# The last stage of a fused eight-stage kernel: expert products in two rounded parts each, the down product turned round

## The chip, the cores and the metric

The kernel is one program on one core of a Trainium2 chip. The time is that of the device, in microseconds (us), for one execution. Several executions are timed, and one more is recorded by the hardware profiler, which gives the trace that is read here.

## The reference

A residual stream x of 4 x 512 = 2048 tokens by 128 passes through eight layers, each `x = x + layer(layernorm(x))`: gated linear attention, a routed feed-forward layer, low-rank attention, a second routed layer, a block with generated weights, a ternary feed-forward layer, full attention with 16 heads, and a mixture of experts. Only the last one is changed. It has 8 experts with 512 slots each, and every token goes to its two best experts:

```
scores = softmax(xt @ wg);  gates_k, idx_k = top_k(scores, 2), gates normalized to sum 1
disp[e, slot] += token rows, in order of choice and token; rows past 512 slots are dropped
h   = relu(einsum('ecd,edh->ech', disp, w1) + b1)     # 128 -> 512
out = einsum('ech,ehd->ecd', h, w2) + b2              # 512 -> 128
y   = sum over k of gates_k * out[idx_k, slot]
```

## The kernel before

The eight stages run one after the other. Residual rows stay in on-chip memory (`sh.x`); each stage has a block of instructions for every engine, in an order written out by hand, and the engines meet through semaphores: `then_inc` counts up when an instruction is done, `wait_ge` holds an engine's queue until a count is reached. Everything behind a wait on the same engine waits too.

The last stage is `dispatched_ffn` (L3051). Its course:

- *Routing.* Layer norm, logits (`route`), softmax and the choice of two experts, and counts that give every token its slot (`give_slots`, `keep`), by all engines for four chunks of tokens. The two expert weight matrices and b2, repeated over the partitions, are loaded at the stage's start by three transfers (L3132 to L3134).
- *Dispatch.* GpSimd issues 32 indirect transfers (L3167) that put rows of 128 tokens each into the slots in device memory (`disp`).
- *Expert loop.* For each expert e, SyncE loads its 512 rows (L3140). TensorE turns them (`turn`, L3228, four transposes of 128x128 in full precision), ScalarE copies the result to `rowsT` (L3275). `up(e)` (L3237) has four products, one for each 128 of the 512 hidden columns: w1's 128x128 stands in the array, 512 turned rows stream through. Full precision needs two records for each such product in the trace. ScalarE applies bias and relu (L3281) from one of two banks `ps_up` into `hidden`. `down(e)` (L3247) has sixteen smaller products, in which 128x128 of the hidden values stand and 128 columns of w2 stream, so that the result has the slots on the partitions. VectorE adds b2 (L3393) and GpSimd stores the 512 rows with four indirect transfers (L3182), to the places by token that VectorE has worked out (L3390, L3391).
- TensorE's order is up(0), turn(1), up(1), turn(2), down(0), up(2), turn(3), down(1), and so on to up(7), down(6), down(7). VectorE's order for each expert is places, then the y of this expert.
- *End.* When all stores have landed SyncE loads the rows back (L3146), VectorE adds them by their gates to the residual (L3402), and the last block stores x.

Of the kernel before, what the change touches and what calls it, by code (L numbers as in the profile page):

```python
# [19 lines left out]
P = 128  # L20
# [3029 lines left out]

def dispatched_ffn(sh, stage, n_exp=8, hid=512, top=2):  # L3051

# [8 lines left out]
    U = top * NT  # L3061
    n_up, n_slot = hid // P, cap // P
    assert cap == S
    GROUP, K16 = 4, top * n_exp
    with ExitStack() as ctx:  # L3065
# [5 lines left out]
        ps_y = [bank(f"y{i}") for i in range(2)]  # L3071
        ps_route, ps_count = [bank("route"), ps_up[0]], [bank("count"), ps_up[1]]
        ROW = D + 1
# [8 lines left out]
        second = sb("second_choice", [P, n_exp, n_slot])  # L3082
        place = sb("place", [P, 2, n_slot])
        place_i = sb("place_int", [P, 2, n_slot], U32)
        tri = sb("tri", [P, P], BF16)
# [21 lines left out]
        rows = sb("rows", [P, 3, n_slot, ROW])  # L3107
        rowsT = sb("rowsT", [P, 2, S])
        hidden = sb("hidden", [P, 2, n_up, S])
        y = sb("y", [P, 2, n_slot, D])  # L3110
        back = sb("back", [P, U, D])
        w1, w2 = sb("w1", [P, n_exp * hid]), sb("w2", [P, n_exp * hid])
        b2 = sb("b2", [P, n_exp * D])
        s_w1, s_w2 = sem("w1_loaded"), sem("w2_b2_loaded")
        s_const = sem("constants_made")
# [12 lines left out]
        @block.sync  # L3128
        def _(sp):
            sh.load_next(sp, stage)  # L3130
            n = n_exp * hid
            sp.dma_start(w1[:, :], sh.extra[stage][:, 0:n]).then_inc(s_w1, 16)  # L3132
            sp.dma_start(w2[:, :], sh.extra[stage][:, n:2 * n]).then_inc(s_w2, 16)
            sp.dma_start(b2[:, :], sh.extra[stage][:, 2 * n:]).then_inc(s_w2, 16)  # L3134
            sp.wait_ge(s_put, 16 * U)
            for e in range(n_exp):
                if e >= 3:
                    sp.wait_ge(s_turn, e - 2)
                    sp.wait_ge(s_placed, e - 2)
                sp.dma_start(rows[:, e % 3, :, :], disp[e * cap:(e + 1) * cap].rearrange(  # L3140
                    "(t p) d -> p t d", p=P)).then_inc(s_rows[e % 3], 16)
            for half in s_out:
                sp.wait_ge(half, 16 * n_slot * n_exp // 2)
            for g in groups:
                at = g * GROUP
                sp.dma_start(back[:, at:at + GROUP, :], outs[at * P:(at + GROUP) * P].rearrange(  # L3146
                    "(t p) d -> p t d", p=P)).then_inc(s_back[g], 16)

        @block.gpsimd
        def _(pool):  # L3150
# [27 lines left out]
            for e in range(n_exp):  # L3178
                pool.wait_ge(s_placed, e + 1)
                pool.wait_ge(s_y, e + 1)  # L3180
                for i in range(n_slot):
                    nc.gpsimd.indirect_dma_start(outs, bass.IndirectOffsetOnAxis(ap=place_i[:, e % 2, i:i + 1], axis=0),  # L3182
                                                 y[:, e % 2, i, :], None).then_inc(s_out[e % 2], 16)

        @block.tensor
        def _(pe):
# [44 lines left out]
            def up(e):  # L3231
                pe.wait_ge(s_rowsT, e + 1)
                for f in range(n_up):
                    m = e * n_up + f
                    if m >= 2:
                        pe.wait_ge(s_hidden, m - 1)
                    nc.tensor.matmul(ps_up[m % 2][:, :], w1[:, m * P:(m + 1) * P], rowsT[:, e % 2, :],  # L3237
                                     start=True, stop=True).then_inc(s_up, 1)

            def down(e):  # L3240
                pe.wait_ge(s_hidden, (e + 1) * n_up)
                if e >= 2:
                    pe.wait_ge(s_y, e - 1)
                for i in range(n_slot):
                    for f in range(n_up):
                        m = e * n_up + f
                        last = nc.tensor.matmul(ps_y[e % 2][:, i * P:(i + 1) * P], hidden[:, e % 2, f, i * P:(i + 1) * P],  # L3247
                                                w2[:, m * D:(m + 1) * D], start=(f == 0 and i == 0),
                                                stop=(f == n_up - 1), skip_group_check=True)
                last.then_inc(s_down, 1)  # L3250

            turn(0)
            pe.wait_ge(s_w1, 16)
            pe.wait_ge(s_w2, 32)
            for e in range(n_exp):
                up(e)
                if e + 1 < n_exp:
                    turn(e + 1)
                if e >= 1:
                    down(e - 1)  # L3260
            down(n_exp - 1)

        @block.scalar
        def _(act):
            act.wait_ge(sh.wsem[stage], 16)
            for c in range(B):
# [3 lines left out]
                nc.scalar.activation(mine, mine, ACT.Exp).then_inc(s_exp, 1)  # L3270
            for e in range(n_exp):
                act.wait_ge(s_turn, e + 1)
                if e >= 2:
                    act.wait_ge(s_up, (e - 1) * n_up)
                nc.scalar.copy(rowsT[:, e % 2, :], ps_t[e % 2][:, :]).then_inc(s_rowsT, 1)  # L3275
                for f in range(n_up):
                    m = e * n_up + f
                    act.wait_ge(s_up, m + 1)
                    if e >= 2 and f == 0:
                        act.wait_ge(s_down, e - 1)  # L3280
                    nc.scalar.activation(hidden[:, e % 2, f, :], ps_up[m % 2][:, :], ACT.Relu,  # L3281
                                         bias=w["b1"][:, m:m + 1]).then_inc(s_hidden, 1)

        @block.vector
        def _(dve):
# [98 lines left out]
            at.then(nc.vector.tensor_scalar(second[:, :, :], second[:, :, :], float(T), None, ALU.mult))  # L3384
            dve.wait_ge(s_w2, 32)
            for e in range(n_exp):
                dve.wait_ge(s_rows[e % 3], 16 * (e // 3 + 1))
                if e >= 2:
                    dve.wait_ge(s_out[e % 2], 16 * n_slot * (e // 2))
                at.then(nc.vector.tensor_tensor(place[:, e % 2, :], rows[:, e % 3, :, D], second[:, e, :], ALU.add))  # L3390
                nc.vector.tensor_copy(place_i[:, e % 2, :], place[:, e % 2, :]).then_inc(s_placed, 1)  # L3391
                dve.wait_ge(s_down, e + 1)
                nc.vector.tensor_tensor(y[:, e % 2, :, :], ps_y[e % 2][:, :].rearrange("p (t d) -> p t d", t=n_slot),  # L3393
                                        b2[:, e * D:(e + 1) * D].unsqueeze(1).broadcast_to([P, n_slot, D]),
                                        ALU.add).then_inc(s_y, 1)
            at.end()
# [93 lines left out]
def _layout(stage, a):  # L3490
# [39 lines left out]
    if stage == 7:  # L3530
        down = a["w2"].reshape(8, 4, P, D).transpose(2, 0, 1, 3).reshape(P, -1)
        return [("wg", a["wg"]), ("b1", a["b1"].reshape(-1, P).T),
                ("extra", cat(a["w1"].transpose(1, 0, 2).reshape(D, -1), down, _rows(a["b2"])))]
    if stage == 5:
# [37 lines left out]
```

## Time and profile before

| what | value |
|---|---|
| median of 3 runs | 1720.01 us (1719.81 to 1721.59) |
| the profiled execution | 1717.78 us, span of its trace 1715.7 us |
| TensorE busy over the span | 1390.8 us, 81% |
| VectorE, ScalarE, GpSimd busy | 1088.0, 748.9, 740.5 us |
| mean granted TensorE clock | 0.882 of full |
| the last stage | from about 1558 us to the end |

The span is the time from the first to the last instruction of the recorded execution; what the execution takes beside it is 2.1 us. The last stage is under a tenth of the whole. Times in the trace are given from the span's start. A weight load into TensorE (PEld) lies beside the products (PE), and the record of a product reaches beyond the start of the next one, so that the distance of two starts says what one costs.

### The profile page before, as it was taken

To read this page: it belongs to the slowest core of one execution; us is meant where nothing else is said; L and a number is where in the kernel's file an instruction comes from. 1 tells how busy PE (TensorE), PEld (TensorE's weight loads), DVE (VectorE), ACT (ScalarE), POOL (GpSimd) and SP (SyncE) were. 2 spreads that over 40 slices of the span, in tenths; PEclk is the share of its full clock that TensorE was granted. 3 is DMA by queue.
4 is the path that set the end of the run, shared out by engine and by line. 5 is a ranking of instruction groups with operands and counts; after the bars stand their busy time and mean duration, and the time that the engine had idled before them with its cause. 6 is when DMAs were issued, how large, how long until landed. Compare 5 with 4: busy or idle time off the path is not lost. (4 is left out here: it accounts for less than half of the span.)

```text
span 1715.7 us, 24915 instructions
## 1 busy us (share of the span) xinstructions
PE 1390.8 (81%) x8900; PEld 844.5 (49%) x8907; DVE 1088.0 (63%) x2898; ACT 748.9 (44%) x1168; POOL 740.5 (43%) x795
## 2 busy tenths in 40 slices
PE   4586578879998793899978899799999999985193
PEld 2354556554444462444435677554555545534062
DVE  6766588667886547688843332578778777756212
ACT  3554244325666143366644333355455454430040
POOL 4442345442223545422233543255546465563533
PEclk9688689958999796599988999999999999996597
DMA  2000005020000124000001020000000000003213
GB/s 92 11 7 2 33 1 210 0 84 1 2 1 1 49 63 173 1 2 1 2 1 46 7 99 1 1 1 1 1 1 1 1 1 1 1 1 123 62 52 97
DMA packets 29562, 52.74 MB, mean 31 GB/s; under 512 B 3216, under 2 KB 24592, under 8 KB 27264
## 3 DMA queue, kind: packets, MB, share of 16 engines
q1 hardware_dynamic: 26144, 44.36, 7.3%
q0 software_dynamic: 3296, 6.78, 1.2%
q8 instruction: 73, 1.20, 0.3%
q14 instruction: 49, 0.40, 0.1%
HBM read 29.07 MB, written 21.02 MB: 29 GB/s over the span
## 5 line engine op out<-in xcount | busy, mean ns | idle before, releaser
L2392 DVE CUSTOM_DVE_ANT_0 s_masked_scores<-s_for_max,s_mask_qk 128x128 bf16<-128x128 f32 (+3 forms) x512 | 227.2, 487 | 59.9 <-PE s_for_max L2216 58.1
L2825 POOL TENSOR_TENSOR wbuf<-s_probs 128x1024 f32<-128x1024 f32 x64 | 151.9, 2374 | 205.3 <-ACT s_probs L2984 205.3
L2984 ACT ACTIVATE s_probs<-s_scores 128x1024 f32<-128x1024 f32 x128 | 132.2, 1033 | 201.7 <-PE s_scores L2906 201.7
L2168 POOL TENSOR_SCALAR_AFFINE_SELECT s_probs<-s_probs 128x256 f32<-128x256 f32 x256 | 100.9, 407 | 271.4 <-ACT s_probs L2323 157.3
L3026 DVE TENSOR_REDUCE s_negmax<-s_for_max 128x2 f32<-128x1024 f32 x126 | 152.2, 1208 | 20.0 <-PE s_for_max L2881 20.0
L2216 PE MATMUL s_for_max<-s_k_stack,s_q_stack 32*128 32x128 f32 (+3 forms) x512 | 142.7, 443 | 27.2 <-DVE s_max_wide L2392 17.5
L3033 DVE RECIPROCAL s_recip<-s_pv_and_sums 128x128 f32<-128x128 f32 x128 | 116.7, 934 | 47.3 <-PE s_pv_and_sums L2932 47.3
L2216 PEld LDWEIGHTS s_for_max<-s_k_stack,s_q_stack 32*128 32x128 f32 x512 | 72.3, 206 | 129.6 <-DVE s_max_wide L2392 89.1
L2323 ACT ACTIVATE s_probs<-s_scores 128x1024 f32<-128x1024 f32 x128 | 127.3, 1024 | 18.2 <-PE s_scores L2237 18.0
L2919 PE MATMUL s_pv_and_sums<-s_probs,s_v 128*64 128x512 f32 x512 | 123.9, 605 | 0.9 <-DVE wbuf L3041 0.9
L2251 PE MATMUL s_pv<-s_probs,s_v_and_one 128*32 128x512 f32 (+3 forms) x1024 | 95.0, 465 | 1.5 <-DVE s_o L2411 1.5
L2310 ACT ACTIVATE s_low_rows_hi<-s_odd_jobs,s_low_rows_bias,s_low_rows 128x512 fp32r<-128x512 f32 x64 | 49.7, 777 | 102.9 <-PE s_odd_jobs L2196 102.1
L2237 PE MATMUL s_scores<-s_q_stack,s_k_stack 32*128 32x512 f32 (+3 forms) x512 | 82.8, 401 | 0.7 <-ACT s_probs L2323 0.7
L2830 POOL TENSOR_TENSOR xnT<-wbuf 128x1024 f32<-128x1024 f32 x32 | 78.2, 2444 | 2.5
L1242 POOL TENSOR_TENSOR s_hidden_lo<-s_hidden,s_hidden_hi 128x512 fp32r<-128x512 f32 x36 | 49.4, 1373 | 56.1 <-ACT s_hidden_hi L1353 56.1
L1899 POOL TENSOR_TENSOR s_h_lo<-s_h,s_h_hi 128x512 fp32r<-128x512 f32 x32 | 42.5, 1330 | 71.0 <-DVE s_h_hi L1993 71.0
L2906 PE MATMUL s_scores<-s_q_hi,s_k_hi 64*128 64x512 f32 x256 | 63.8, 494 | 9.6 <-ACT s_probs L2984 9.6
L2906 PEld LDWEIGHTS s_scores<-s_q_hi,s_k_hi 64*128 64x128 f32 x256 | 23.8, 183 | 77.2 <-issue 56.2
L2919 PEld LDWEIGHTS s_pv_and_sums<-s_probs,s_v 128*64 128x64 f32 x512 | 31.2, 136 | 61.4 <-issue 61.4
L2881 PE MATMUL s_for_max<-s_k_hi,s_q_hi 64*128 64x512 f32 x252 | 50.6, 396 | 1.9 <-DVE s_negmax L3026 1.1
L2906 PE MATMUL s_scores<-s_q_lo,s_k_hi 64*128 64x512 f32 x256 | 51.0, 393 | 0.0
L3182 POOL DMA_INDIRECT expert_rows<-s_y,s_place_int x32 | 30.6, 958 | 47.1 <-DVE s_place_int L3391 39.5
(574 smaller groups left out, 3449.8 us busy)
## 6 DMA issues: line engine op xcount, KB each, us to landing
rows_by_expert<-s_empty_rows SPq DMA_DIRECT2D x8, 1032.0 KB, 10.4
s_w<-extra SPq DMA_DIRECT2D x2, 2048.0 KB, 9.8
wbuf<-w SPq DMA_DIRECT2D x1, 3460.0 KB, 11.2
s_probs<-extra SPq DMA_DIRECT2D x1, 2898.0 KB, 10.1
wbuf<-w SPq DMA_DIRECT2D x1, 2888.0 KB, 14.1
wbuf<-w SPq DMA_DIRECT2D x1, 2124.0 KB, 7.9
dispatched<-s_empty_slots SPq DMA_DIRECT2D x1, 2064.0 KB, 8.5
s_rows<-dispatched SPq DMA_DIRECT2D x8, 258.0 KB, 2.7
```

The lines of the kernel that those rows point to most:

```text
L2168: last = nc.gpsimd.affine_select(out=diag, in_=diag, compare_op=ALU.is_ge, fill=0.0, base=0, pattern=[[0, diag.shape[1]], [1, P]], channel ...
L2216: last = nc.tensor.matmul(p1[m % 2][:, at:at + n], stacks[0][rows, q % SLOTS, i * P:n], stacks[1][rows, q % SLOTS, 0:n], start=True, stop= ...
L2237: last = nc.tensor.matmul(p2[n % 2][:, at:at + S - j * P], stacks[1][rows, q % SLOTS, j * P:(j + 1) * P], stacks[0][rows, q % SLOTS, j * P ...
L2251: last = nc.tensor.matmul(po[32 * x:32 * x + 32, j * P:S], v32[:, c % 2, j, 4 * g + x, :], probs[:, q % 2, slab, at:at + S - j * P], start ...
L2323: nc.scalar.activation(probs[:, q % 2, r, :], p2[n % 2][:, :], ACT.Exp, scale=scale).then_inc(s_exp, 1)
L2392: last = nc.vector.tensor_tensor_reduce(out=junk[:, m % 2, at:at + n], in0=p1[m % 2][:, at:at + n], in1=mask[:, S - n:S], scale=1.0, scala ...
L2825: nc.gpsimd.tensor_tensor(added[half], probs[:, g % 2, 2 * half, :, :], probs[:, g % 2, 2 * half + 1, :, :], ALU.add).then_inc(s_added, 1)
L2906: last = nc.tensor.matmul(p2[:, x, :], kp, qp, start=(part == 0), stop=(part == 3))
L2919: last = nc.tensor.matmul(po[x * dh:(x + 1) * dh, :], v[:, c % 2, j, (2 * n + x) * dh:(2 * n + x + 1) * dh], probs[:, g % 2, j, x, :], sta ...
L2984: nc.scalar.activation(probs[:, g % 2, j, :, :], p2[:, :, :], ACT.Exp, scale=dh ** -0.5).then_inc(s_exp, 1)
L3026: nc.vector.tensor_reduce(negmax[:, g % 2, :, j], max_bank(g, j)[:, :, :], AX.X, ALU.max, negate=True).then_inc(s_neg, 1)
L3033: nc.vector.reciprocal(recip[:, at], ps_sum[:, at]).then_inc(s_rec, 1)
```

## The change

All matrices of the expert products are split into a high part, rounded to the type float32r, and a low part, the rest, also as float32r. A product of full precision is replaced by three of rounded parts that are added up in the same bank: high by high, low weight by high value, high weight by low value.

- The weights are loaded whole into the two weight buffers that the earlier stages used. ScalarE makes the high parts in 16 pieces of 128x512 behind its last exponential, VectorE the low parts behind the routing; TensorE's first `up` waits for all of them.
- Turned rows: ScalarE copies the high part, VectorE subtracts for the low one.
- Hidden values: ScalarE writes relu's result to one of two buffers `hidden`, then copies the high part (`high`), and VectorE subtracts (`low`). High and low parts have eight buffers each (DEEP).
- The down product is turned round: w2 stands, 512 slots stream through, and the result `yT` has the features on the partitions. VectorE takes it out with b2 as a value for each partition (`take_yT`), TensorE transposes it back with four transposes (`turn_y`), VectorE copies it to y (`take_y`).
- TensorE's order in round e is up(e), turn(e+1), turn_y(e-2), down(e-1), for ten rounds, where what doesn't exist is left out. VectorE's is places of e, low parts 0 to 2, low part of the next rows, low part 3, take_y(e-2), take_yT(e-1).
- Places have four buffers instead of two; b2 comes with the small weights and no longer repeated.

```diff
+        ps_turned_y = [bank("route"), bank("count")]
+        ps_route, ps_count = [ps_turned_y[0], ps_up[0]], [ps_turned_y[1], ps_up[1]]
         ROW = D + 1
...
+        DEEP = 2 * n_up
+        rowsT = [sb(f"rowsT_{m}", [P, 2, S], F32R) for m in ("hi", "lo")]
+        hidden = sb("hidden", [P, 2, S])
+        hid = [sb(f"hidden_{m}", [P, DEEP, S], F32R) for m in ("hi", "lo")]
+        yT = sb("yT", [P, S])
         y = sb("y", [P, 2, n_slot, D])
-        back = sb("back", [P, U, D])
-        w1, w2 = sb("w1", [P, n_exp * hid]), sb("w2", [P, n_exp * hid])
-        b2 = sb("b2", [P, n_exp * D])
-        s_w1, s_w2 = sem("w1_loaded"), sem("w2_b2_loaded")
+        w_cols = n_exp * f_all
+        w_lo, w_hi = sb("w_lo", [P, 2 * w_cols], F32R), sb("w_hi", [P, 2 * w_cols], F32R)
+        w_chunks = 2 * w_cols // S
+        own = sh.weights[stage][0].shape[1]
+        whole = [sh.wbuf[(list(sh.weights).index(stage) + 1) % 2][:, 0:w_cols],
+                 sh.wbuf[list(sh.weights).index(stage) % 2][:, own:own + w_cols]]
+        back = whole[1].rearrange("p (u d) -> p u d", d=D)
+
+        def whole_chunk(k):
+            half, at = divmod(k * S, w_cols)
+            return whole[half][:, at:at + S]
+
+        s_w = [sem("w1_loaded"), sem("w2_loaded")]
+        s_whi, s_wlo = sem("w_hi_ready"), sem("w_lo_ready")
+        s_rhi, s_hhi, s_hlo, s_yT, s_yturn = (sem("rowsT_hi_ready"), sem("hidden_hi_ready"), sem("hidden_lo_ready"),
...
-            sp.dma_start(w1[:, :], sh.extra[stage][:, 0:n]).then_inc(s_w1, 16)
-            sp.dma_start(w2[:, :], sh.extra[stage][:, n:2 * n]).then_inc(s_w2, 16)
-            sp.dma_start(b2[:, :], sh.extra[stage][:, 2 * n:]).then_inc(s_w2, 16)
+            for k in range(2):
+                sp.dma_start(whole[k],
+                             sh.extra[stage][:, k * w_cols:(k + 1) * w_cols]).then_inc(s_w[k], 16)
             sp.wait_ge(s_put, 16 * U)
...
                         pe.wait_ge(s_hidden, m - 1)
-                    nc.tensor.matmul(ps_up[m % 2][:, :], w1[:, m * P:(m + 1) * P], rowsT[:, e % 2, :],
-                                     start=True, stop=True).then_inc(s_up, 1)
+                    at = slice(m * P, (m + 1) * P)
+                    nc.tensor.matmul(ps_up[m % 2][:, :], w_hi[:, at], rowsT[0][:, e % 2, :], start=True, stop=False)
+                    nc.tensor.matmul(ps_up[m % 2][:, :], w_lo[:, at], rowsT[0][:, e % 2, :], start=False, stop=False)
+                    nc.tensor.matmul(ps_up[m % 2][:, :], w_hi[:, at], rowsT[1][:, e % 2, :], start=False,
+                                     stop=True).then_inc(s_up, 1)
 
             def down(e):
-                pe.wait_ge(s_hidden, (e + 1) * n_up)
+                if e >= 2:
+                    pe.wait_ge(s_yT, e - 1)
+                for f in range(n_up):
+                    m = e * n_up + f
+                    pe.wait_ge(s_hlo, m + 1)
+                    at = slice(w_cols + m * P, w_cols + (m + 1) * P)
+                    nc.tensor.matmul(ps_y[e % 2][:, :], w_hi[:, at], hid[0][:, m % DEEP, :], start=(f == 0), stop=False)
+                    nc.tensor.matmul(ps_y[e % 2][:, :], w_lo[:, at], hid[0][:, m % DEEP, :], start=False, stop=False)
+                    last = nc.tensor.matmul(ps_y[e % 2][:, :], w_hi[:, at], hid[1][:, m % DEEP, :], start=False,
+                                            stop=(f == n_up - 1))
+                last.then_inc(s_down, 1)
+
+            def turn_y(e):
+                pe.wait_ge(s_yT, e + 1)
                 if e >= 2:
                     pe.wait_ge(s_y, e - 1)
                 for i in range(n_slot):
-                    for f in range(n_up):
-                        m = e * n_up + f
-                        last = nc.tensor.matmul(ps_y[e % 2][:, i * P:(i + 1) * P], hidden[:, e % 2, f, i * P:(i + 1) * P],
-                                                w2[:, m * D:(m + 1) * D], start=(f == 0 and i == 0),
-                                                stop=(f == n_up - 1), skip_group_check=True)
-                last.then_inc(s_down, 1)
+                    last = nc.tensor.transpose(ps_turned_y[e % 2][:, i * P:(i + 1) * P], yT[:, i * P:(i + 1) * P],
+                                               sh.ident[:, :])
+                last.then_inc(s_yturn, 1)
 
             turn(0)
-            pe.wait_ge(s_w1, 16)
-            pe.wait_ge(s_w2, 32)
-            for e in range(n_exp):
-                up(e)
+            pe.wait_ge(s_wlo, w_chunks)
+            for e in range(n_exp + 2):
+                if e < n_exp:
+                    up(e)
                 if e + 1 < n_exp:
                     turn(e + 1)
-                if e >= 1:
+                if e >= 2:
+                    turn_y(e - 2)
+                if 1 <= e <= n_exp:
                     down(e - 1)
-            down(n_exp - 1)
 
         @block.scalar
         def _(act):
@@ -3268,18 +3297,34 @@
                 act.wait_ge(s_less, c + 1)
                 mine = probs[:, c * TPC:(c + 1) * TPC, :]
                 nc.scalar.activation(mine, mine, ACT.Exp).then_inc(s_exp, 1)
-            for e in range(n_exp):
+            for k in range(w_chunks):
+                act.wait_ge(s_w[2 * k // w_chunks], 16)
+                nc.scalar.copy(w_hi[:, k * S:(k + 1) * S], whole_chunk(k)).then_inc(s_whi, 1)
+
+            def rows_high(e):
                 act.wait_ge(s_turn, e + 1)
                 if e >= 2:
                     act.wait_ge(s_up, (e - 1) * n_up)
-                nc.scalar.copy(rowsT[:, e % 2, :], ps_t[e % 2][:, :]).then_inc(s_rowsT, 1)
+                nc.scalar.copy(rowsT[0][:, e % 2, :], ps_t[e % 2][:, :]).then_inc(s_rhi, 1)
+
+            def high(m):
+                if m >= DEEP:
+                    act.wait_ge(s_down, (m - DEEP) // n_up + 1)
+                act.wait_ge(s_hidden, m + 1)
+                nc.scalar.copy(hid[0][:, m % DEEP, :], hidden[:, m % 2, :]).then_inc(s_hhi, 1)
+
+            rows_high(0)
+            for e in range(n_exp):
                 for f in range(n_up):
                     m = e * n_up + f
                     act.wait_ge(s_up, m + 1)
-                    if e >= 2 and f == 0:
-                        act.wait_ge(s_down, e - 1)
-                    nc.scalar.activation(hidden[:, e % 2, f, :], ps_up[m % 2][:, :], ACT.Relu,
+                    if m >= 2:
+                        act.wait_ge(s_hlo, m - 1)
+                    nc.scalar.activation(hidden[:, m % 2, :], ps_up[m % 2][:, :], ACT.Relu,
                                          bias=w["b1"][:, m:m + 1]).then_inc(s_hidden, 1)
+                    if f == n_up - 1 and e + 1 < n_exp:
+                        rows_high(e + 1)
+                    high(m)
 
...
-            dve.wait_ge(s_w2, 32)
-            for e in range(n_exp):
+            for k in range(w_chunks):
+                dve.wait_ge(s_whi, k + 1)
+                cs = slice(k * S, (k + 1) * S)
+                nc.vector.tensor_tensor(w_lo[:, cs], whole_chunk(k), w_hi[:, cs].bitcast(F32),
+                                        ALU.subtract).then_inc(s_wlo, 1)
+
+            def rows_low(e):
+                dve.wait_ge(s_rhi, e + 1)
+                nc.vector.tensor_tensor(rowsT[1][:, e % 2, :], ps_t[e % 2][:, :], rowsT[0][:, e % 2, :].bitcast(F32),
+                                        ALU.subtract).then_inc(s_rowsT, 1)
+
+            def low(m):
+                dve.wait_ge(s_hhi, m + 1)
+                nc.vector.tensor_tensor(hid[1][:, m % DEEP, :], hidden[:, m % 2, :], hid[0][:, m % DEEP, :].bitcast(F32),
+                                        ALU.subtract).then_inc(s_hlo, 1)
+
+            def place_of(e):
                 dve.wait_ge(s_rows[e % 3], 16 * (e // 3 + 1))
+                if e >= 4:
+                    dve.wait_ge(s_out[e % 2], 16 * n_slot * (e // 2 - 1))
+                at.then(nc.vector.tensor_tensor(place[:, e % 4, :], rows[:, e % 3, :, D], second[:, e, :], ALU.add))
+                nc.vector.tensor_copy(place_i[:, e % 4, :], place[:, e % 4, :]).then_inc(s_placed, 1)
+
+            def take_yT(e):
+                dve.wait_ge(s_down, e + 1)
+                if e:
+                    dve.wait_ge(s_yturn, e)
+                nc.vector.tensor_scalar(yT[:, :], ps_y[e % 2][:, :], w["b2"][:, e:e + 1], None,
+                                        ALU.add).then_inc(s_yT, 1)
+
+            def take_y(e):
+                dve.wait_ge(s_yturn, e + 1)
                 if e >= 2:
                     dve.wait_ge(s_out[e % 2], 16 * n_slot * (e // 2))
-                at.then(nc.vector.tensor_tensor(place[:, e % 2, :], rows[:, e % 3, :, D], second[:, e, :], ALU.add))
-                nc.vector.tensor_copy(place_i[:, e % 2, :], place[:, e % 2, :]).then_inc(s_placed, 1)
-                dve.wait_ge(s_down, e + 1)
-                nc.vector.tensor_tensor(y[:, e % 2, :, :], ps_y[e % 2][:, :].rearrange("p (t d) -> p t d", t=n_slot),
-                                        b2[:, e * D:(e + 1) * D].unsqueeze(1).broadcast_to([P, n_slot, D]),
-                                        ALU.add).then_inc(s_y, 1)
+                nc.vector.tensor_copy(y[:, e % 2, :, :], ps_turned_y[e % 2][:, :].rearrange(
+                    "p (t d) -> p t d", t=n_slot)).then_inc(s_y, 1)
+
+            rows_low(0)
+            for e in range(n_exp + 2):
+                if e < n_exp:
+                    place_of(e)
+                    for f in range(n_up - 1):
+                        low(e * n_up + f)
+                    if e + 1 < n_exp:
+                        rows_low(e + 1)
+                    low(e * n_up + n_up - 1)
+                if e >= 2:
+                    take_y(e - 2)
+                if 1 <= e <= n_exp:
+                    take_yT(e - 1)
```

## Rows read from the trace of the kernel before

**Rows 1.** Three stretches: length, busy us of each engine, granted clock, DMA share, GB/s.

```profile
1480.00:1500.00 20.00, 19.24 (x106) 9.51 (x106) 15.34 (x18) 10.31 (x15) 12.04 (x6) 1.00 0.00 1
1622.00:1626.00 4.00, 3.06 (x7) 1.66 (x8) 0.34 (x2) 0.58 (x1) 0.00 (x0) 0.50 0.64 170
1643.00:1685.00 42.00, 42.00 (x257) 30.48 (x256) 5.17 (x16) 16.56 (x26) 21.07 (x22) 1.00 0.19 56
```

**Rows 2.** The chain of waits in the expert loop: start us, us, what.

```profile
1624.05 5.90 PE s_up L3237 x8
...
1631.19 3.89 PE s_up L3237 x8
...
1639.09 3.62 PE s_up L3237 x8
1642.71 0.44 PE s_turned L3228 x4
...
1677.26 3.62 PE s_up L3237 x8
...
1694.78 2.23 DMA expert_rows<-s_y,s_place_int
```

**Rows 3.** The timeline at the loop's end, DVE and POOL: start us, us, engine, line.

```profile
1677.30 0.69 DVE L3393 TENSOR_TENSOR s_y<-s_y,s_b 128x512 f32<-128x512 f32 x1 [6.67 <-PE s_y L3247]
...
1678.74 0.96 POOL L3182 DMA_INDIRECT expert_rows<-s_y,s_place_int  x1 [2.89 <-DVE s_place_int L3391]
...
1685.94 0.96 POOL L3182 DMA_INDIRECT expert_rows<-s_y,s_place_int  x1 [2.46 <-DVE s_place_int L3391]
...
1694.78 0.96 POOL L3182 DMA_INDIRECT expert_rows<-s_y,s_place_int  x1 [0.30 <-issue]
```

**Rows 4.** The timeline of the stage before (full attention), PE and ACT.

```profile
1486.83 1.02 ACT L2984 ACTIVATE s_probs<-s_scores 128x1024 f32<-128x1024 f32 x1 [3.07 <-PE s_scores L2906]
...
1487.91 0.50 PE L2906 MATMUL s_scores<-s_q_hi,s_k_hi 64*128 64x512 f32 x2 [0.63 <-ACT s_probs L2984]
...
1492.49 0.50 PE L2785 MATMUL s_odd_jobs<-s_xnT_hi,s_wq_hi 128*128 128x512 f32 x1
...
1492.83 0.39 PE L2785 MATMUL s_odd_jobs<-s_xnT_hi,s_wq_lo 128*128 128x512 f32 x1
...
1493.06 0.39 PE L2785 MATMUL s_odd_jobs<-s_xnT_lo,s_wq_hi 128*128 128x512 f32 x1
```

**Rows 5.** Groups over the whole span: count, busy us, mean ns.

```profile
L1353 ACT CAST s_hidden_hi<-s_hidden 128x512 fp32r<-128x512 f32 x36 | 22.2, 616 | 19.3 <-DVE s_hidden L1426 19.2
...
L221 DVE TENSOR_TENSOR s_xnT_lo<-xnT,s_xnT_hi 128x512 fp32r<-128x512 f32 x10 | 6.8, 685 | 0.9 <-ACT xnT L261 0.9
```

**Rows 6.** The timeline of the expert loop, ACT.

```profile
1623.33 0.58 ACT L3275 COPY s_rowsT<-s_turned 128x512 f32<-128x512 f32 x1 [36.23 <-PE s_turned L3228]
...
1629.98 0.69 ACT L3281 ACTIVATE s_hidden<-s_up,wbuf 128x512 f32<-128x512 f32 x1 [0.17 <-PE s_up L3237]
1630.57 0.58 ACT L3275 COPY s_rowsT<-s_turned 128x512 f32<-128x512 f32 x1
...
1639.99 0.69 ACT L3281 ACTIVATE s_hidden<-s_up,wbuf 128x512 f32<-128x512 f32 x1 [3.71 <-PE s_up L3237]
...
1640.85 0.69 ACT L3281 ACTIVATE s_hidden<-s_up,wbuf 128x512 f32<-128x512 f32 x1 [0.17 <-PE s_up L3237]
```

**Rows 7.** The timeline of the dispatch, ACT, POOL and DVE.

```profile
1586.87 0.23 ACT L3270 ACTIVATE s_probs<-s_probs 128x32 f32<-128x32 f32 x1 [4.80 <-DVE s_probs L3295]
...
1592.93 1.07 POOL L3167 DMA_INDIRECT dispatched<-s_xn,s_idx  x1 [1.37 <-DVE s_idx L3323]
...
1594.31 0.95 POOL L3167 DMA_INDIRECT dispatched<-s_xn,s_idx  x1 [0.30 <-issue]
...
1594.88 0.43 DVE L3367 TENSOR_TENSOR s_weighted<-s_chosen,s_probs 128x256 f32<-128x256 bf16 x1
...
1597.29 0.18 DVE L3384 TENSOR_SCALAR s_second_choice<-s_second_choice 128x32 f32<-128x32 f32 x1
...
1617.03 0.95 POOL L3167 DMA_INDIRECT dispatched<-s_xn,s_idx  x1 [0.30 <-issue]
```

More of the change, by code:

```diff
@@ L3048, in _, with dispatched_ffn @@
                                             ALU.add).then_inc(s_x, 1)
-def dispatched_ffn(sh, stage, n_exp=8, hid=512, top=2):
+def dispatched_ffn(sh, stage, n_exp=8, f_all=512, top=2):
     nc, w, tag = sh.nc, sh.w(stage), f"s{stage}"
@@ L3061, in dispatched_ffn @@
     U = top * NT
-    n_up, n_slot = hid // P, cap // P
+    n_up, n_slot = f_all // P, cap // P
     assert cap == S
@@ L3071, in dispatched_ffn @@
         ps_y = [bank(f"y{i}") for i in range(2)]
-        ps_route, ps_count = [bank("route"), ps_up[0]], [bank("count"), ps_up[1]]
+        ps_turned_y = [bank("route"), bank("count")]
+        ps_route, ps_count = [ps_turned_y[0], ps_up[0]], [ps_turned_y[1], ps_up[1]]
         ROW = D + 1
@@ L3082, in dispatched_ffn @@
         second = sb("second_choice", [P, n_exp, n_slot])
-        place = sb("place", [P, 2, n_slot])
-        place_i = sb("place_int", [P, 2, n_slot], U32)
+        place = sb("place", [P, 4, n_slot])
+        place_i = sb("place_int", [P, 4, n_slot], U32)
         tri = sb("tri", [P, P], BF16)
@@ L3107, in dispatched_ffn @@
         rows = sb("rows", [P, 3, n_slot, ROW])
-        rowsT = sb("rowsT", [P, 2, S])
-        hidden = sb("hidden", [P, 2, n_up, S])
-        y = sb("y", [P, 2, n_slot, D])
-        back = sb("back", [P, U, D])
-        w1, w2 = sb("w1", [P, n_exp * hid]), sb("w2", [P, n_exp * hid])
-        b2 = sb("b2", [P, n_exp * D])
-        s_w1, s_w2 = sem("w1_loaded"), sem("w2_b2_loaded")
+        DEEP = 2 * n_up
[3 more added lines that the diff above has]
+        yT = sb("yT", [P, S])
+        y = sb("y", [P, 2, n_slot, D])
+        w_cols = n_exp * f_all
[11 more added lines that the diff above has]
+        s_rhi, s_hhi, s_hlo, s_yT, s_yturn = (sem("rowsT_hi_ready"), sem("hidden_hi_ready"), sem("hidden_lo_ready"),
+                                              sem("yT_ready"), sem("y_transposed"))
         s_const = sem("constants_made")
@@ L3130, in _ @@
             sh.load_next(sp, stage)
-            n = n_exp * hid
-            sp.dma_start(w1[:, :], sh.extra[stage][:, 0:n]).then_inc(s_w1, 16)
-            sp.dma_start(w2[:, :], sh.extra[stage][:, n:2 * n]).then_inc(s_w2, 16)
-            sp.dma_start(b2[:, :], sh.extra[stage][:, 2 * n:]).then_inc(s_w2, 16)
+            for k in range(2):
+                sp.dma_start(whole[k],
+                             sh.extra[stage][:, k * w_cols:(k + 1) * w_cols]).then_inc(s_w[k], 16)
             sp.wait_ge(s_put, 16 * U)
@@ L3181, in _ @@
                 for i in range(n_slot):
-                    nc.gpsimd.indirect_dma_start(outs, bass.IndirectOffsetOnAxis(ap=place_i[:, e % 2, i:i + 1], axis=0),
+                    nc.gpsimd.indirect_dma_start(outs, bass.IndirectOffsetOnAxis(ap=place_i[:, e % 4, i:i + 1], axis=0),
                                                  y[:, e % 2, i, :], None).then_inc(s_out[e % 2], 16)
@@ L3531, in _layout @@
         down = a["w2"].reshape(8, 4, P, D).transpose(2, 0, 1, 3).reshape(P, -1)
-        return [("wg", a["wg"]), ("b1", a["b1"].reshape(-1, P).T),
-                ("extra", cat(a["w1"].transpose(1, 0, 2).reshape(D, -1), down, _rows(a["b2"])))]
+        return [("wg", a["wg"]), ("b1", a["b1"].reshape(-1, P).T), ("b2", a["b2"].T),
+                ("extra", cat(a["w1"].transpose(1, 0, 2).reshape(D, -1), down))]
     if stage == 5:
```

## The prediction

> **What bounds the kernel now.** I read the stretches of the last stage first [rows 1], with each engine's busy time and the granted clock. From 1643 to 1685 us TensorE (PE) is busy for all 42.00 us at clock 1.00, while VectorE (DVE), ScalarE (ACT) and GpSimd (POOL) are busy for 5.17, 16.56 and 21.07: the expert loop is bound by PE. The chain of waits [rows 2] gives the loop's beat: up(2) starts at 1639.09, up(7) at 1677.26, so 38.17 us for five experts, 7.63 each: 3.62 for the four up products, 0.44 for four transposes, and the rest, 3.57, for the down products. The end is bound by something else, seen on the POOL queue [rows 3]: y(5) is ready at 1677.30 + 0.69, its four stores start at 1678.74, y(6)'s start at 1685.94, and from there eight follow every 1.263 us ((1694.78 - 1685.94) / 7) to the last at 1694.78. y(7)'s stores don't wait for their y. So what sets the end is when POOL gets its last y's: POOL needs 5.05 us an expert, and anything that makes y late near the end is paid in full. After the last issue come its 2.23 us landing, the loads back and the sums, which the change leaves alone.
>
> **The change, part by part.**
>
> *Products.* A full-precision 128x512 product costs 3.62 / 4 = 0.905 us [rows 2]. A rounded one is started 0.23 after the one before (1492.83 to 1493.06) where the operands are there, and 0.34 where PE had just stood (1492.49 to 1492.83): 0.11 more for a restart [rows 4]. Three parts are 0.70. Up: 4 x 0.70 = 2.78; down: the same, in place of 3.57; two sets of transposes: 0.88. PE's work in one expert falls from 7.63 to 6.45.
>
> *Can the others keep up?* ACT now does, per product, the relu (0.687) and the rounded copy of its result. For that copy the nearest row is 0.616 [rows 5]; neighbours on ACT overlap by 0.10 (1629.98 to 1630.57 for a relu of 0.69 [rows 6]), but the copy reads what the relu wrote, so I give it 0.04 after the relu's end; bounds 0 and 0.14 (ACT to PE, 1623.33 + 0.58 to 1624.05 [rows 2, 6]); I take it near the lower, because PE follows ACT within 0.06 where its weights are at hand (1486.83 + 1.02 to 1487.91 [rows 4]). So ACT's beat is 0.69 + 0.04 + 0.61 - 0.10 = 1.24 a product, against PE's 0.70. DVE subtracts: 0.685 for one [rows 5].
>
> One expert from the start of up(e), with 0.16 from PE's last column to ACT (two up products of 0.905 from 1639.09 end at 1640.90, ACT's second relu starts at 1640.85, its first at 1639.99; 0.06 to 0.16, the latter taken [rows 2, 6]) and the 0.06 from ACT back to PE: products 0 and 1 end at 1.39. Relu 0 runs 0.86 to 1.55, so product 2 goes from 1.61 to 2.41 with its restart. Copy 0 ends at 2.20, relu 1 runs 2.10 to 2.79, product 3 goes 2.85 to 3.65. Then transposes of rows (e+1) to 4.09, of yT (e-2) to 4.53, down(e-1) to 7.32. ACT meanwhile: relu 3 ends at 5.27, the high part of the next rows at 5.75, the last copy at 6.26; DVE: low part of the next rows 5.81 to 6.50, last low part 6.40 to 7.09. The next up(e+1) needs the rows at 6.56, before 7.32. The added waits that aren't last: relu m waits for the low part of m-2 (copy 0 ends at 2.20, subtracted by 2.93, relu 2 starts at 3.34). DVE stands for down(e-1) until 7.48; queued behind are yT (to 8.28, 0.96 in the next round), the places (to 1.3) and the next low part 0, whose copy ends only at 2.20. **The beat is 7.32, not 6.45**: PE stands 0.22 + 0.11 and 0.44 + 0.11 us behind relu 0 and relu 1. Bounds: 6.45 (nothing stands) and 7.9 (the hand-overs behind ACT, some seven in the chain, 0.14 instead of 0.04 to 0.06).
>
> *Start of the loop.* up(0) waits for the rows' low part as well: 0.06 + 0.69 later, at 1624.8. The clock is 0.50 there [rows 1], half of the full rate, so a product costs double, 3 x 0.46 = 1.4. Relus start at about 1626.4, 1627.6, 1628.8 and 1630.1, on ACT's beat of 1.24 by then; next rows' high part to 1631.2, low part to 1631.97, up(1) at 1632.03, against 1631.19. From there 3.65 + 0.44 + 2.79 = 6.88 (no turned y yet): up(2) at 1638.9 against 1639.09. If the clock rises some us later than before (up(1), 3.89 us, ran at full speed but for a stand), ACT's chain hides all but about 0.4. up(7): 1638.9 + 5 x 7.32 = 1675.5, which is 1.75 us earlier than before.
>
> *The y's come one round later.* Before, y(5) was taken right after down(5), at the start of round 7. Now DVE takes yT(5) there, PE turns it in round 7 behind up(7), and DVE takes it behind the low parts of round 7. In that round (no next rows) copy 3 ends at 5.92, the last low part at 6.67, y(5) at 7.27: 1675.5 + 7.27 = 1682.8, against 1677.99, so 4.8 us late. POOL starts 0.76 behind it (1677.99 to 1678.74), at 1683.55, and is free then: y(4) is ready at 1668.2 + 7.69 = 1675.9, its stores over by 1681.7. The 12 last stores now run in one piece if y(6) and y(7) are ready in time. y(6): down(6) ends at 6.88, yT taken to 7.86, turned to 8.4, y at 9.3; POOL wants it at 8.03 + 5.05 = 13.1. y(7): down(7) to 11.2, yT to 12.1, turned to 12.7; its buffer is free when y(5)'s stores have landed, 8.03 + 3 x 1.263 + 0.96 + 2.23 = 15.0; y at 15.7, store from 16.5; POOL wants it at 18.1. Both in time. Last issue: 1683.55 + 11 x 1.263 = 1697.45, against 1694.78: **+2.67 us**. The beat's bounds put it 4.4 us earlier or 2.9 later. In other terms: y(5) comes 7.27 us behind the start of up(7) where it came 0.73 behind (1677.99 - 1677.26), 6.54 more; 1.75 of that PE wins back, and 2.15 is POOL's pause before y(6) (1685.94 - 1678.74 - 4 x 1.263), which is gone: 6.54 - 1.75 - 2.15 = 2.64, the same but for rounding.
>
> *Splitting the weights.* 16 copies on ACT behind its last exponential (1586.87 + 0.23), 16 x 0.52 = 8.3 us, over by 1596; 16 subtractions on DVE behind 1597.29 + 0.18, 16 x 0.69 = 11 at most, over by 1609. up(0) wants them at 1624: the dispatches on POOL, to 1617.99, and the rows' way back hide them [rows 7]. Without that cover it would be 19 us.
>
> *Does DVE's splitting slow POOL's issues?* Two dispatches ran while DVE was at work on SBUF, the second beside a two-input instruction of 0.43 us: 1.07 and 0.95 us, against 0.95 with DVE idle (1617.03) [rows 7]. So 0 to 0.12 for each of about 9: 0 to 1.1 us, and I take 0, since the second is the nearer case. What a subtraction of 0.69 could do is rival D.
>
> *Small edits.* The load of b2 (512 KB) goes; it was issued beside w1 and w2 at the stage's start, 60 us before PE wants it: 0. Bias b2 per partition, four place buffers instead of two, place(e) moved ahead (0.33 us): 0; the cover is DVE's idle time, still some 2 us in each round (its seven 128x512 instructions and the places take 7 x 0.69 + 0.33 = 5.2 of 7.32), and without it 0.3 a round. Bounds of all together -0.3 to +0.3.
>
> **Sum.** Profiled execution 1717.78 (span 1715.7) + 2.7 = 1720.5. The median of the runs is 1720.01, 2.2 above the profile, so 1722.7 for the runs. What a measurement can tell from no change is 0.2%, 3.4 us; the forecast lies inside it.
>
> **Rivals.**
> A. *The hand-overs on ACT and DVE cost more, and the loop gives nothing.* If the beat comes to 7.6 or more, up(7) starts 1.4 us or more later than I say: +4.1 and up, 1724.1 to 1726. It decides from a beat of 7.47 on ((3.44 - 2.67) / 5 = 0.15 above mine), or where the start of the loop loses 0.8; the price is then 5 us per us of beat. For it: ACT to itself, ACT to DVE and DVE back to PE in each product, where before there was only ACT to PE. Against: DVE has 2 us to spare in each round. 25 in 100.
> B. *PE runs at its own work.* If relus don't hold it and the beat is 6.55, up(7) starts at 1671.7; y(5) at about 6 behind it; last issue 1677.7 + 0.76 + 13.9 = 1692.3: -2.5, 1717.5. Even this isn't faster by 0.2%. For it: the copy could be put behind the next relu only by another order in the code, which isn't there. 8 in 100; with start and order gains on top, -3.5, a few in 100.
> C. *The clock falls in the loop.* In the stage before, PE stood 0.63 us ahead of a group of products (1487.91) and kept clock 1.00 [rows 1, 4]; here it stands 0.9 us in 7.3. At half clock a round is 24 x 0.46 + 1.76 = 12.8: six rounds, +33: 1755. The Trainium skill (TensorE: Matmul & The Clock Gate, A second HAM failure mode) tells of a kernel whose short stands between PSUM groups made the clock swing; this trace doesn't show it. 3 in 100.
> D. *POOL's issues wait for DVE's subtractions.* If an issue had to wait for a whole subtraction, 9 dispatches x 0.69 = 6.2 us come on top: +8.9, 1728.9. For it: one of the two took 1.07. Against: the other took 0.95 [rows 7]. The Trainium skill (SBUF — State Buffer, Who interferes with whom) says that a DVE instruction with two SBUF inputs contends only with what GpSimd reads, and infers that writing descriptors isn't that; by that rule D falls out, and the trace agrees with 0.95 us. 4 in 100.
>
> **How the numbers follow.** Forecast 60 in 100, its own range 1721.0 to 1723.4, where A begins. Faster: 6, the best end of B. Slower: A, C and D, 32. Same: the forecast and the rest of B, 62. The range for 8 in 10 reaches to B and into A and D: 1718.5 to 1727.
>
> **What would show it.** Right: rounded products every 0.23 us, two stands a round, a beat near 7.3; y(5) some 7 us behind up(7); twelve stores in one piece at the end, the last issued near 1697.5. Wrong: a beat above 7.5 or under 7; POOL idle between the last stores; dispatches longer than 0.96 between 1597 and 1609; a granted clock under 1.00 after 1632.

## The result, and the profile after

In 20 runs of each the changed kernel took 1726.6 us (median), the kernel before 1720.17. The ratio is 1.0031 [1.0018, 1.0044], 5.3 us slower (3.1 to 7.6). The forecast of 1722.7 was 3.9 low, outside its own range (1721.0 to 1723.4) and inside that for 8 in 10. Its sign was right; I had put "within 0.2%" first (62 in 100) and "slower" second (32).

The profiled execution took 1730.78 us, 13.0 more than that of before. Most of this isn't the change: the last stage starts at 1569.24 instead of 1558.82, behind code that is the same. Starts move by as much from trace to trace (experiments), so I measure inside the stage: **from its first layer-norm statistics to the last issue of a store, and to the end**. Before: 1694.78 - 1558.82 = 135.96 and 156.88; after: 139.57 and 159.46.

The stretches of the changed kernel, as in [rows 1]:

```profile
1593.00:1622.00 29.00, 2.16 (x23) 1.98 (x23) 21.96 (x71) 8.53 (x17) 20.14 (x21) 0.50 0.14 47
1643.00:1685.00 42.00, 39.50 (x181) 29.38 (x182) 26.77 (x50) 31.07 (x53) 16.18 (x16) 1.00 0.17 48
1685.00:1700.00 15.00, 12.36 (x56) 8.88 (x55) 8.29 (x14) 5.72 (x10) 8.86 (x10) 1.00 0.12 39
```

PE's share in the loop falls from 42.00 of 42 to 39.50 of 42, DVE's rises from 5.17 to 26.77 and ACT's from 16.56 to 31.07; the clock stays at 1.00. One round and the end, from the chain of waits and the timeline:

```profile
1672.15 0.23 PE s_up L3253
...
1672.87 0.70 ACT s_hidden L3323
1673.68 0.48 issue
1674.16 0.69 ACT s_hidden L3323
1674.90 0.50 PE s_up L3253
...
1675.87 0.44 PE s_turned L3243 x4
1676.30 0.44 PE s_count L3276 x4
1676.74 0.23 PE s_y L3265
...
1680.21 0.70 ACT s_hidden L3323
```

```profile
1686.50 0.69 DVE L3464 COPY s_y<-s_route 128x512 f32<-128x512 f32 x1
...
1687.94 0.96 POOL L3197 DMA_INDIRECT expert_rows<-s_y,s_place_int  x1 [2.19 <-DVE s_y L3464]
...
1688.31 0.62 ACT L3314 CAST s_hidden_hi<-s_hidden 128x512 fp32r<-128x512 f32 x1
...
1688.83 0.68 ACT L3323 ACTIVATE s_hidden<-s_up,wbuf 128x512 f32<-128x512 f32 x1
...
1693.45 0.68 DVE L3464 COPY s_y<-s_count 128x512 f32<-128x512 f32 x1
...
1694.89 0.96 POOL L3197 DMA_INDIRECT expert_rows<-s_y,s_place_int  x1 [1.82 <-DVE s_y L3464]
...
1708.81 0.96 POOL L3197 DMA_INDIRECT expert_rows<-s_y,s_place_int  x1 [0.31 <-issue]
```

Round 5 starts with up(5) at 1672.15, and up(7) follows at 1686.81: a beat of 7.33, against 7.63 [rows 2]. Products start every 0.23 us. PE stands twice, behind relu 0 and relu 1 (the chain's two "ACT s_hidden"); relu 1 (1674.16) stands behind copy 0, as the timeline shows two rounds later (copy 0 at 1688.31 + 0.62, relu 1 at 1688.83). Where a product follows without a stand, the chain puts its start 0.16 later than the timeline (up(7): 1686.81 and 1686.65); starts of up are the chain's here, unless the timeline is named. In the last full round y(5) is ready at 1693.45 + 0.68, and from 1694.89 twelve stores go out in one piece, the last at 1708.81. The y of the round before is taken at 1686.50, 7.0 us behind its up(6), and its first store goes at 1687.94, since POOL waits for y and places.

### The profile page after: what moved, and what is told of

The parts are those of the page before. It is cut to its first block and busy times, and to the rows that moved or that the text cites. A ratio compares the mean times of both kernels' runs of the same rounds, so it can differ in the third digit from the quotient of the medians.

```text
span 1728.7 us, 24906 instructions
## 1 busy us (share of the span) xinstructions
PE 1402.3 (81%) x8811; PEld 851.0 (49%) x8811; DVE 1129.6 (65%) x2962; ACT 775.1 (45%) x1216; POOL 742.8 (43%) x795
## 5 line engine op out<-in xcount | busy, mean ns | idle before, releaser
L2251 PE MATMUL s_pv<-s_probs,s_v_and_one 128*32 128x512 f32 (+3 forms) x1024 | 99.6, 485 | 1.5 <-DVE s_o L2411 1.5
L2237 PE MATMUL s_scores<-s_q_stack,s_k_stack 32*128 32x384 f32 (+3 forms) x512 | 84.1, 410 | 0.3 <-ACT s_probs L2323 0.3
```

What stands on the lines that cost most here:

```text
L2237: last = nc.tensor.matmul(p2[n % 2][:, at:at + S - j * P], stacks[1][rows, q % SLOTS, j * P:(j + 1) * P], stacks[0][rows, q % SLOTS, j * P ...
L2251: last = nc.tensor.matmul(po[32 * x:32 * x + 32, j * P:S], v32[:, c % 2, j, 4 * g + x, :], probs[:, q % 2, slab, at:at + S - j * P], start ...
```

## The experiments

All numbers of a loop are from one trace each. The beat is the mean distance of the starts of up from up(3) to up(7). "Last issue" (of a store) and "end" count from the stage's start; 156.04 is the mean end of the three traces of before.

| kernel | start of the stage | beat | last issue | end | end against before (156.04) | measured, from the ratio |
|---|---|---|---|---|---|---|
| before, three traces | 1558.82, 1564.17, 1560.80 | 7.63 | 135.96, 135.53, 136.15 | 156.88, 155.53, 155.70 | | |
| changed, first | 1569.24 | 7.34 | 139.57 | 159.46 | +3.4 | +5.3 (3.1 to 7.6) |
| changed, again | 1562.33 | 7.35 | 139.87 | 159.87 | +3.8 | +5.7 (1.9 to 9.5) |
| y before the next rows | 1569.92 | 7.36 | 138.50 | 158.58 | +2.5 | +1.5 (-2.1 to 5.2) |
| y turned inside up | 1566.82 | 6.93 | 133.44 | 153.98 | -2.1 | -2.6 (-6.4 to 1.0) |
| relus in pairs | 1560.75 | 6.74 | 136.77 | 156.95 | +0.9 | +1.9 (-1.0 to 4.8) |
| both | 1554.28 | 6.53 | 131.25 | 151.02 | -5.0 | -4.6 (-7.6 to -1.7) |
| changed, 44 products ahead | 1556.63 | 7.34 | 139.49 | 160.17 | +4.1 | +2.9 (0 to 5.9) |
| both, 44 products ahead | 1557.34 | 6.53 | 130.56 | 150.36 | -5.7 | -4.8 (-7.6 to -2.1) |
| both, 60 products | 1564.11 | 6.56 | 130.73 | 150.59 | -5.4 | -4.1 (-7.7 to -0.3) |

The last column is (ratio - 1) times 1720, with its 95% interval.

**Both kernels again**, unchanged (e0_before_again, e9_before_third, e1_after_again).

> The kernel before, unchanged, for a second trace of it. Measured by the last stage alone, from its first layer-norm statistics to the last issue of a store (135.96 us in the first trace of before, 139.57 in that of after) and from there to the end of the span (20.9 and 19.9). Theory T (what the change does is in the last stage: the y's come one round later and the queue of stores pays): again 136.0 and 20 to 21, while the stage's start moves by some us either way. Rival U (the change also costs time in the stages ahead of it, whose code is the same): the start of the last stage is at 1558 to 1560 again, against 1569 in the trace of after.

> The kernel before, unchanged, for a third trace. Theory T: 135.5 to 136.0 us to the last issue of a store, 155.5 to 157 to the end, while the stage's start differs from the other two traces of it by some us. Rival U: its start lies under every start of a changed kernel measured on the same chip.

> The changed kernel, unchanged, for a second trace. Theory T: last stage again 139.2 to 139.6 us to the last issue, and the stage's start anywhere between 1556 and 1570. Rival U: the stage's start again near 1569, 8 to 10 us behind that of the kernel before.

The traces of one kernel agree within 0.6 us at the last issue and within 1.4 at the end; the two kernels lie 3.8 us apart at the last issue (means 135.88 and 139.72), 3.6 at the end. Two last issues came just above what I had said, by 0.15 (136.15) and 0.27 (139.87). The starts of the stage go from 1554 to 1570 over twelve traces whose code ahead is the same, and on one chip that of the kernel before (1564.17) lies between those of changed ones (1562.33, 1569.92, 1566.82). On the chip of the third trace it lies under that of the one changed kernel there (1560.80, 1564.11), as rival U said; one pair can't tell. Rival U falls as a cost of 8 to 10 us. In nine comparisons the ratio and the stage's own difference agree within the interval; the ratios lie on the mean 0.5 us higher, so a cost of some 1 us ahead of the stage is neither shown nor excluded.

**The place of y's taking** (e2_y_before_rows).

```diff
                     for f in range(n_up - 1):
                         low(e * n_up + f)
+                if e >= 2:
+                    take_y(e - 2)
...
-                if e >= 2:
-                    take_y(e - 2)
```

> VectorE takes the turned y between low part 2 and the next rows' low part instead of behind low part 3; nothing else. Theory T: y(5) is ready 1.3 us earlier in its round, the twelve last stores still run in one piece, so the last issue comes 1.3 us earlier: 138.2 us for the stage; the beat stays 7.33. Rival H (ACT's hand-overs in the loop set the end): the stage stays at 139.5.

The start of up(7) and the first store of y(5), from the timeline:

```profile
1687.58 0.39 PE L3253 MATMUL s_up<-s_rowsT_hi,s_w_hi 128*128 128x512 f32 x1
...
1694.53 0.96 POOL L3197 DMA_INDIRECT expert_rows<-s_y,s_place_int  x1 [1.81 <-DVE s_y L3464]
```

The store goes 6.95 us behind up(7) instead of 8.24 (1694.89 - 1686.65), and the last issue comes at 138.50, 1.2 us less than the changed kernel at the same beat: the end follows y(5), and nothing in the loop's pace needed to change. This is the trace's evidence; the measured times alone (+1.5 and +5.3, with intervals that overlap) don't tell the two kernels apart.

**The transposes inside up** (e4_turn_inside_up); VectorE's take_y moved to behind place_of.

```diff
                 for f in range(n_up):
+                    if f == 2 and e >= 2:
+                        turn_y(e - 2)
...
-                if e >= 2:
+                if e >= n_exp:
                     turn_y(e - 2)
```

> TensorE transposes y(e-2) between products 1 and 2 of up(e), where it stands for relu 0, and VectorE takes it at the round's start. Theory T: the beat falls by the 0.44 us of the transposes to 6.9, y(5) comes 2.7 us behind the start of up(7) instead of 7.3, and the stores then wait for y(6): last issue 18.4 us behind the start of up(7) instead of 22.0, the start itself 2.2 earlier: 133.8 us for the stage, 5.8 less than the changed kernel and 2.2 less than the kernel before. Rival H: the beat stays 7.3, and only the earlier y(5) counts: 136 us.

The beat was 6.93 and the last issue 133.44, where I had said 6.9 and 133.8. This is 6.3 us less than the changed kernel (mean of its two traces), although the numbers of instructions are the same on all engines.

**Relus in pairs** (e3_relu_pairs); the next rows' low part ahead of low parts 2 and 3.

```diff
-                    high(m)
+                    if f % 2:
+                        high(m - 1)
+                        high(m)
```

> ScalarE does two relus and then the two high copies, instead of relu and copy in turn, and VectorE takes the next rows' low part before low parts 2 and 3; else the changed kernel. Theory T: relu 1 no longer stands behind copy 0, so product 3 follows product 2 without a stand, and the beat falls from 7.34 to 6.8 us; y(5) comes some 0.4 later in its round, since the last low parts are later: last issue of a store at 137.2 us of the stage (139.6 and 139.9 in the two traces of the changed kernel). Rival: the beat is set by hand-overs as such, whose number is the same, and stays 7.3.

The beat was 6.74 (6.8 said) and the last issue 136.77, 0.4 less than expected. The stand behind relu 1 was one of order, not of hand-overs as such, whose number is unchanged.

**Both** (e5_both).

> The transposes of y inside up, and the relus in pairs, together. Theory T: both stands of TensorE are gone, the beat is TensorE's own work, 6.45 to 6.55 us, and y(5) comes early in its round: last issue at 130.5 us of the stage, 3 less than with the transposes inside up alone and 5 less than the kernel before (135.5 and 136.0). Rival: VectorE or ScalarE becomes the bound, beat 6.9 as in the experiment before: 133.4.

The ratio is 0.9973 [0.9956, 0.999]: faster than the kernel before, by 0.27%. A round in the timeline, two sets of transposes at its ends:

```profile
1644.31 0.60 PE L3243 MATMUL s_turned<-ident,s_rows 128*128 128x128 f32 x4
1644.56 1.38 POOL L3197 DMA_INDIRECT expert_rows<-s_y,s_place_int  x1 [1.36 <-DVE s_y L3468]
...
1648.38 1.37 ACT L3325 ACTIVATE s_hidden<-s_up,wbuf 128x512 f32<-128x512 f32 x2 [0.97 <-PE s_up L3257]
...
1649.01 0.66 PE L3278 MATMUL s_route<-ident,s_yT 128*128 128x128 f32 x4
...
1649.42 0.48 PE L3255 MATMUL s_up<-s_rowsT_hi,s_w_hi 128*128 128x512 f32 x1
...
1650.89 0.60 PE L3243 MATMUL s_turned<-ident,s_rows 128*128 128x128 f32 x4
```

From 1644.31 to 1650.89 and to 1657.38, 6.58 and 6.49; the products run without a stand, but the one behind either set of transposes takes 0.1 us more (1649.42). The last issue came 0.75 later than I said (131.25, 130.5 said). The last eight stores wait for y(6), 0.76 us after y(5)'s are over; so y(5)'s longer stores, up to 1.35 us instead of 0.96, are not what delays the end. Nor is the stretch behind up(7): the last issue lies 18.39 us behind its start in the timeline (1685.53 - 1667.14), where I had said 18.4 with the transposes inside up. So most of the 0.75 lies ahead of up(7).

**Products ahead of the loop**, with and without the two edits; they add nothing to the result (e6_warm, e7_all, e8_warm_through).

```diff
-            turn(0)
             pe.wait_ge(s_wlo, w_chunks)
+            for k in range(44):
+                nc.tensor.matmul(ps_y[k % 2][:, :], w_hi[:, 0:P], w_lo[:, 0:S], start=True, stop=True)
+            turn(0)
```

> The changed kernel with 44 products into banks not yet in use, on TensorE, between the making of the weights' low parts and the first transposes (they add nothing to the result), so that the granted clock is 1.00 when the loop starts. Theory T: the distance from the first set of transposes to the second falls from 7.87 to about 6.4 us, the rest of the loop is as before, and the last issue of a store comes at 138.3 us of the stage. Rival: the clock at the loop's start is hidden behind ScalarE, as I argued for all but 0.4 us: 139.3.

> The two edits of the order and the 44 products ahead of the loop. Theory T: 129.2 us to the last issue of a store, the whole 6 us under the kernel before, ratio 0.996. Rival: what the loop's start gives back is lost at the stores, which want their 5.06 us an expert: no less than with the two edits alone.

> The two edits of the order, with 55 products ahead of the first transposes and 5 between them and up(0), which add nothing to the result, so that TensorE doesn't stand before the loop as it did for 3.0 and 1.4 us in the run with 44. Theory T: the clock stays at 1.00 through up(0), the distance from the first to the second set of transposes is 5.5 us (6.55 with 44 products, 7.09 with none), and the last issue of a store comes at 129.9 us of the stage (130.56 and 131.25). Rival: ScalarE's chain hides the clock at the start, and nothing moves against the run with 44.

Stretches of the run with 60 (columns as in [rows 1]), and six of its instructions; behind them, two of the run with both edits and 44 products:

```profile
1630.00:1633.00 3.00, 2.92 (x12) 2.00 (x13) 0.29 (x2) 2.13 (x4) 0.00 (x0) 1.00 0.37 88
1633.00:1640.00 7.00, 4.58 (x16) 3.38 (x15) 3.33 (x8) 5.10 (x10) 0.00 (x0) 0.76 0.16 40
```

```profile
1627.80 0.66 PE L3243 MATMUL s_turned<-ident,s_rows 128*128 128x128 f32 x4 [0.53 <-DMA s_rows<-dispatched]
...
1629.86 0.50 PE L3255 MATMUL s_up<-s_rowsT_hi,s_w_hi 128*128 128x512 f32 x1 [0.25 <-DVE s_rowsT_lo L3448]
...
1633.11 0.60 PE L3243 MATMUL s_turned<-ident,s_rows 128*128 128x128 f32 x4
1636.12 0.50 PE L3255 MATMUL s_up<-s_rowsT_hi,s_w_hi 128*128 128x512 f32 x1 [2.42 <-DVE s_rowsT_lo L3448]
1636.46 0.46 PE L3256 MATMUL s_up<-s_rowsT_hi,s_w_lo 128*128 128x512 f32 x1
1636.72 0.63 PE L3257 MATMUL s_up<-s_rowsT_lo,s_w_hi 128*128 128x512 f32 x1
```

```profile
1630.14 0.51 PE L3255 MATMUL s_up<-s_rowsT_hi,s_w_hi 128*128 128x512 f32 x1 [2.41 <-DVE s_rowsT_lo L3444]
...
1630.72 0.40 PE L3257 MATMUL s_up<-s_rowsT_lo,s_w_hi 128*128 128x512 f32 x1
```

With 44 products and the order unchanged, TensorE stood 2.35 us before the first transposes and 1.40 before up(0), and the clock was back at 0.50 (1.2 GHz) in most of up(0). The distance from the first to the second transposes was 7.31 us where I had said 6.4, and the last issue 139.49 where I had said 138.3: nothing was won, and the rival (139.3) had it. With both edits and 44 products the last issue was 130.56, 1.4 later than I said (129.2), and the ratio 0.9972 (0.996 said); against both edits alone (131.25) that is 0.7 less, about the spread between traces.

With 60, up(0) ran at 1.00 and the first distance fell to 5.31 (5.5 said). But then TensorE stands 2.42 us for the second rows' parts, and the clock fell to 0.50 within the second product of up(1) (0.46 us; the third took 0.63). The second distance rose from 6.26 (44 products) to 7.48, so that the two together are the same, 12.81 and 12.79. The last issue is 130.73 against 130.56, where I had said 129.9. The rival had the number, though not the reason: what up(0) won was given back in up(1).

The stand alone doesn't decide that. TensorE stands 2.41 us at the same place with both edits and no products, and with 44, and there the clock stayed at 1.00 (third product 0.40 us); with the order unchanged and 44 products a stand of 2.03 us there was followed by products of 0.63. What tells these apart is open.

## Why the prediction was nearly right, point by point

- *The products, the beat*: 0.23 and 0.34 as read, beat 7.34 against 7.32. Right, and for the right reason: pairing the relus takes the stand behind relu 1 away.
- *The split of the weights, POOL's dispatches*: ACT's copies were over at 1605.70 (36.5 us into the stage), DVE's subtractions at 1618.01, and the dispatches beside the subtractions took 0.96 each. Both are hidden: the last dispatch is over 59.1 us into the stage (1628.37), 59.2 before. Rival D had nothing there.
- *The y's one round later*: y(5) 7.32 us behind up(7) (1694.13 - 1686.81), 7.27 said; POOL 0.76 behind; twelve stores in one piece. Right.
- *The start of the loop* is the term that was mis-sized: up(2) came 17.43 us after the first transposes (1650.13 - 1632.70), 16.73 said (1638.9 - 1622.17). 0.42 of it lies before up(1). I had spaced the relus of up(0) by ScalarE's own 1.24 us, named a later rise of the clock as worth "about 0.4", and added nothing for it. The clock did rise later: some 9 us behind the first transposes (0.80 between 1641 and 1642, below), where in the kernel before it was some 6 (0.74 between 1628 and 1629). So up(0) ran at half clock to its end, its relus came every 1.28 us, three rounded products of 0.43 each, and ScalarE waited a little for the next rows' transposes. The rest lies between up(1) and up(2): 0.11 is PE's restart at up(1), which pushed the relus and copies along, and 0.16 depends on how starts are read. By the timeline up(2) is that much earlier, and y(5) then comes 7.48 us behind up(7), not 7.32.
- *The rest*: first transposes 0.2 us later in the stage, beat and queue 0.15 in all. Together 2.67 + 0.70 + 0.35 = 3.7, where the traces show 3.8. At the start of up(7) PE was 0.6 us ahead of before (117.57 us into the stage against 118.19, means of the traces), not 1.75.
- *The time*: of the 3.9 us between forecast and measured, the stage in the traces has 1.1 (3.8 against 2.7). Another 1.5 lies between the traces and the ratio (5.3, with an interval that reaches down to 3.1), and the rest between the ratio and the medians, which are 6.4 apart. Neither has a cause that the runs show.
- *Rivals*: A's result came (slower by over 0.2% in the median), without its mechanism: the beat stayed under its point of 7.47, and the hand-overs cost what I had said. It came by A's other condition, a start of the loop that loses some 0.8 (0.70, and 0.2 more at the first transposes), through the clock. My border between "same" and "slower" lay 0.8 us above the forecast, and the one term that slipped took it across; 32 in 100 was too little for that. B and C did not come: the beat wasn't PE's own work, and the clock stayed at 1.00 from 1643 to 1690.

The start of up(0) in the changed kernel, columns as in [rows 1]:

```profile
1636.00:1640.00 4.00, 4.00 (x11) 3.07 (x10) 1.07 (x2) 2.97 (x5) 0.00 (x0) 0.50 0.27 66
1640.00:1641.00 1.00, 1.00 (x5) 0.71 (x5) 0.41 (x2) 0.97 (x3) 0.00 (x0) 0.50 0.00 0
1641.00:1642.00 1.00, 0.58 (x3) 0.22 (x2) 0.59 (x1) 0.88 (x2) 0.00 (x0) 0.80 0.00 0
1642.00:1644.00 2.00, 1.02 (x4) 0.86 (x5) 1.53 (x4) 0.74 (x3) 0.00 (x0) 1.00 0.00 0
```

## What to carry to other kernels

A queue that is not the bound on the average can still set the end: count back from the last store how long that queue needs for what is still to come, and ask when each piece reaches it. A pipeline with one more round of delay pays that round at the end, and here the whole of PE's gain (0.6 us at the start of up(7), 1.75 forecast) went there and 3.8 more; the same instructions in another order were up to 8.5 us faster at the last issue. A TensorE that is kept warm before a loop may cool at one of the loop's first stands, and then nothing is won. Where an engine stands for another inside a round, put there what has to be done anyway.

## What was not expected of the hardware

POOL's store issues took 0.96 us each in the kernel before and 1.02 on the mean in the changed one, five of the 32 1.27 to 1.31, while its dispatches beside sixteen equally long VectorE subtractions took 0.96 throughout. The row of the stores:

```profile
L3197 POOL DMA_INDIRECT expert_rows<-s_y,s_place_int x32 | 32.7, 1021 | 48.7 <-DVE s_y L3464 40.8 <-issue 7.9
```

Both are beside two-input VectorE instructions from on-chip memory. In both traces of the changed kernel the long one is always the second of an expert's four stores (1689.21 + 1.27, say), and with both edits it is the first. One difference shows in the rows: ScalarE had made its last copy (1605.70) before the subtractions beside the dispatches began (1607.83), while it is at work in the loop. Whether that is the cause wasn't tried and stays open. At the end it costs nothing here, since POOL stands for y(5) behind these stores (1.82 us before 1694.89) and the last twelve took 0.96 each.
